# VectorE's turn of an expert loop: weighted rows and the next-but-one tile's first basis placed ahead of the hidden normalisation

## What is computed

```python
logits = x @ gate_W;  rw, sel = top_k(softmax(logits), 2);  rw = rw / rw.sum(-1)
# experts 0 to 3, "plain"
mlp_out = gelu(x @ mlp_W1 + b1) @ mlp_W2 + b2
# experts 4 to 7, "KAN"
basis0 = rswaf(layernorm(x), grid)          # 8 grid points: 1 - tanh(..)^2
z      = basis0 @ kan_sl_W0 + b0            # 128*8 -> 256
basis1 = rswaf(layernorm(z), grid)          # 256*8
kan_out = basis1 @ kan_sl_W1 + b1           # -> 128
out = sum over experts of w_full[t, e] * expert_out[e, t]
```

## Time and profile before

| | us |
|---|---|
| median of 3 runs (952.75, 953.87, 958.70) | 953.87 |
| the profiled execution | 949.07 |
| its span, first to last instruction | 947.2 |
| mean granted TensorE clock | 0.954 of full speed |

### The profile page before, as it was taken

How to read it: one execution, slowest core, us unless ns; L and a number is a source line. 1 busy time by engine, 2 the same in 40 slices (tenths; PEclk the granted TensorE clock), 3 DMA queues, 4 the chain that set the end, 5 groups by cost and what they waited for, 6 DMA issues and landing times.

```text
span 947.2 us, 23326 instructions
## 1 busy us (share of the span) xinstructions
PE 814.1 (86%) x7978; PEld 627.7 (66%) x7979; DVE 501.0 (53%) x2069; ACT 548.8 (58%) x731; POOL 505.6 (53%) x649
## 2 busy tenths in 40 slices
PE   3699897998979989789896889999889899899980
PEld 1456675666656766657675668888668698677870
DVE  6734726547356373563744664565635845576240
ACT  6566664666656666566565463764835737556330
POOL 6240624546246361463547377676867767766522
PEclk9799998999999999999999989999999999899985
DMA  3302040130401303103047062552634525424213
GB/s 74 97 32 68 2 132 1 36 98 2 130 3 36 98 2 106 26 22 112 2 127 150 19 158 42 135 139 38 135 92 79 138 33 136 120 51 69 21 18 106
DMA packets 91065, 68.24 MB, mean 72 GB/s; under 512 B 42894, under 2 KB 83276, under 8 KB 89038
## 3 DMA queue, kind: packets, MB, share of 16 engines
q1 hardware_dynamic: 74014, 55.11, 20.7%
q0 software_dynamic: 16912, 11.35, 8.5%
HBM read 46.86 MB, written 21.37 MB: 72 GB/s over the span
## 4 chain that ended last, share of the span: by engine, by line
PE 38%; POOL 25%; issue 14%; DVE 9%; ACT 4%; DMA 4%; another core or an unknown queue 1%; SPq 1%; POOLq 1%; DVEq 1%; ACTq 0%
POOL acc_d L752 8%; PE pv L1636 7%; PE pv L1532 5%; PE ring L1598 4%; PE ring L1602 4%; DVE masked L1185 3%; POOL vaug L742 3%; POOL stack L742 3%; PE ring L1498 3%; DMA acc_d<-stack,srec 2%; PE ring L1557 2%; PE ring L1416 2%; ACT Pb L927 2%; POOL zc L768 2%; POOL c L668 2%
## 5 line engine op out<-in xcount | busy, mean ns | idle before, releaser
L752 POOL DMA_INDIRECT acc_d<-stack,srec x84 | 166.6, 1983 | 82.2 <-DVE stack L1104 55.6
L1185 DVE CUSTOM_DVE_ANT_0 masked<-ring,mask_max 128x192 bf16<-128x192 f32 (+1 forms) x512 | 141.2, 337 | 99.1 <-PE ring L1557 87.0
L933 ACT ACTIVATE Pb<-ring 128x768 f32<-128x768 f32 x128 | 101.2, 812 | 78.4 <-PE ring L1586 67.6
L780 POOL TENSOR_SCALAR_AFFINE_SELECT Pb<-Pb 128x1024 f32<-128x1024 f32 x64 | 69.0, 1096 | 125.0 <-ACT Pb L927 124.8
L1116 DVE SCALAR_TENSOR_TENSOR stack<-stack 128x512 f32<-128x512 f32 x160 | 102.1, 688 | 58.3 <-ACT stack L906 55.6
L1498 PE MATMUL ring<-stack 128*128 128x256 f32 x560 | 124.1, 381 | 0.0
L1636 PE MATMUL pv<-Pb,vaug 128*32 128x128 f32 (+3 forms) x2816 | 119.2, 318 | 0.0
L809 POOL DMA_INDIRECT slot_d<-rec,pos x64 | 62.4, 976 | 105.1 <-DVE pos L1287 87.7
L1498 PEld LDWEIGHTS ring<-stack 128*128 128x128 f32 x560 | 105.4, 190 | 19.0 <-issue 5.2
L906 ACT ACTIVATE stack<-ring,kprm 128x512 f32<-128x512 f32 x160 | 108.2, 813 | 0.1
L943 ACT ACTIVATE Pb<-ring 128x768 f32<-128x768 f32 (+1 forms) x128 | 89.0, 758 | 27.7 <-PE ring L1602 26.2
(11 more groups left out here) (243 smaller groups left out, 1374.1 us busy)
## 6 DMA issues: line engine op xcount, KB each, us to landing
stack<-L_ffn_kan_sl_W SPq DMA_DIRECT2D x20, 1024.0 KB, 5.7
stack<-hl_d SPq DMA_DIRECT2D x24, 256.0 KB
stack<-hl_d SPq DMA_DIRECT2D x24, 128.0 KB
stack<-L_ffn_mlp_W SPq DMA_DIRECT2D x12, 256.0 KB
hl_d<-hi SPq DMA_DIRECT2D x7, 384.0 KB, 2.6
hl_d<-lo SPq DMA_DIRECT2D x7, 384.0 KB, 3.5
Pb<-L_ffn_mlp_W SPq DMA_DIRECT2D x10, 256.0 KB
xb<-L_attn_x SPq DMA_DIRECT2D x9, 256.0 KB, 4.7
```

The costliest lines, as they stand in the source:

```text
L752: pool.indirect_dma_start(acc_d, bass.IndirectOffsetOnAxis(ap=srec[:, kind, u % RECS, q, 0:1], axis=0), src[:, u % 2, q, :], None, compute ...
L933: act.activation(Pb[:, n % 2, 2048 + 768 * hd:2048 + 768 * (hd + 1)].rearrange("p (k q) -> p k q", k=2), slot(job)[:, :, 0:384], ACT.Squar ...
L1185: red = dve.tensor_tensor_reduce(masked[:, (NT * n + c) % SLOTS, hh, k0:WQ], slot(job)[:, hh // 2, WQ * (hh % 2) + k0:WQ * (hh % 2 + 1)], ...
```

## The change

VectorE's list of a turn is put in another order, and nothing else: `hidden_norm` of KAN tile u+1 moves behind `weighted(0, ...)` of u+1 and `basis_functions(0, ...)` of u+2, under a condition of its own, so each turn has one condition more on VectorE.

```diff
                         with dve.If(k + 1 < n_kind[1]):
                             hidden_stats(i, u + 1)
-                            hidden_norm(i, u + 1)
                         with dve.If(k + 1 < n_kind[0]):
                             weighted(0, i, u + 1)
                         with dve.If(k + 2 < n_kind[1]):
                             basis_functions(0, i, u + 2)
+                        with dve.If(k + 1 < n_kind[1]):
+                            hidden_norm(i, u + 1)
                         with dve.If(k < n_kind[1]):
                             weighted(1, i, u)
```

## The result

The changed kernel takes 923.42 us (median of 4 runs, 920.82 to 925.51), the kernel before 956.24 with one more run counted, 4 in all (952.75 to 958.70): a ratio of 0.9649, 95% interval 0.9614 to 0.9683, or 33 us less. The profiled execution went from 949.07 to 920.82, 28.2 less, and its span from 947.2 to 919.0. The forecast was 926 us for the median and 919 for the span.

The account below looks back on a forecast made before the run. GpSimd's list was taken to pace turns 3 to 8. A loss of 31.4 us, less 1.8 for short turns and 1.6 for transfers and holds, gave 28 us: profiled 949.07 becomes 921, median 926, range 918 to 940 for eight in ten.

Parts of the forecast that it names:

- The bound before: GpSimd's instruction list, a round of 38.3 us gather to gather, paces turns 3 to 8, which total 230.7 us.
- The sum of 31.4: Turns 1 to 8 took 299.3 us against TensorE's need of 267.9; the 31.4 us loss lies nearly all in turns 3, 4, 5, 7, 8.
- The wait, 3.6 a round: GpSimd's 3.89 us wait for the weighted plain rows shrinks to the usual 0.30 gap, 3.6 us less per round.
- the hold, 3.9 a round: GpSimd's first scatter, held by VectorE's gapless first basis, falls from 5.50 to some 1.6 us, 3.9 less per round.
- The gapless basis in turns 3 and 6: There the first basis stays gapless and holds GpSimd's coefficients or gather, up to 4.4 us, once each.
- Rival A: The hold only moves to a gather or the coefficients; only the wait goes, 21.6 us less, 932 us; chance 0.17.
- TensorE becomes the bound: GpSimd's new round of 30.8 us falls below TensorE's need of 33.3 a turn in turns 3 to 8; clock 1.00.
- need of 267.9: TensorE's own work in turns 1 to 8, summed from fixed matmuls and KAN and plain blocks, 267.9 us.
- short turns, landings and holds: Deductions from the gain: 1.8 us in the two short turns, some 1.6 for transfers and holds longer than 0.1.
- The heads: TensorE's waits at turn heads, 1.91 us for weighted rows and 2.57 for Gelus, both go with the earlier basis.
- The room of the normalisation: Time between the later `hidden_norm` and TensorE's need at the next head; short turns 4 and 7 (-1.2, -0.6) lose 1.8 us.
- rival B: Basis steps each wait for a GpSimd gather or scatter, some 10 us a turn; 975 us, break-even about 7.4; chance 0.06.

Follow-up runs that it names:

- the pair with less matmul: 2 of 16 steps of the second KAN product left out, in the changed order and in the old one: turns 1 to 8 262.8 and 293.6 us.
- gaps_half_weights: Kernel before, with one-element stores between first-basis steps and half of each KAN weight load left out: 278.3 us in turns 1 to 8, ratio 0.9747.
- change_again: The whole change timed again on another chip against the kernel before: 994.16 us against 1021.49, ratio 0.9737, turns 1 to 8 270.1 us.
- The delay experiment: Changed kernel with nine extra VectorE instructions (3.06 us) ahead of each normalisation: 276.8 us in turns 1 to 8, ratio 0.9823 against the kernel before.

## Why the prediction was right

- **The bound before.** GpSimd's round paced turns 3 to 8: right for turns 2 to 7, by the pair with less matmul (0.5 us of 221) and by gaps_half_weights, less so for turn 8.
- **The cuts of the earlier trace rows.** From turn 4 on some cuts lie where TensorE ran out of work and not at the next head: turns 4, 5 and 7 begin at 698.66, 736.91 and 814.57, 2 to 4 us later. Turn 6 was therefore read as fully busy, and it wasn't: 4.23 us of waiting stood at its end. The sum of 31.4 doesn't change by this, only its split over the turns.
- **The wait, 3.6 a round, and the hold, 3.9 a round.** Both went: 0.7 for 3.89, 1.6 to 2.0 for 5.50. The gap left is 0.7 and not 0.3.
- **The gapless basis in turns 3 and 6.** It held one coefficient 4.2 us in turn 6. In turn 3 it held nothing to its end: the coefficients took 0.32 to 0.52 beside it. So my reading of the hold, that it lasts as long as the run is gapless, is right for the scatters and too simple for the coefficients. Rival A's mechanism was there once, without a price, as TensorE had room.
- **TensorE becomes the bound, at full clock.** 268.8 us against a need of 267.9. The 31.4 held both the waits and the slow clock behind them, and both went. The loss left was mis-sized: I had 31.4 - 28 = 3.4 us for short turns, landings and holds, and 0.9 was paid (2.2 in change_again, 1.6 of it at the heads behind the short turns, where I had 1.8). So the loop gained 30.5, and 2 us were lost ahead of turn 1, half of them in turn 0, which I had let keep its time; their cause is open. That the profiled execution came out at 920.82 for a forecast of 921 is luck to that extent: two errors of some 2 us cancel. The median then stood 2.6 above it and not 4.8.
- **The heads.** TensorE's waits for Gelus, 8.6 us in turns 1 to 8 before, are gone, and ScalarE's wait for the basis fell from 64.0 us to 1.4.
- **The room of the normalisation.** Foreseen 6.8, 3.3, 2.9, -1.2, 5, 2.6, -0.6 for turns 1 to 7; the trace after has 6.9, 3.4, 5.3, -0.2, 7.0, 4.4, -0.3. The delay experiment paid exactly where this says. The break-even of rival B was not tried; by the rooms of the prediction it comes to 7.0 us, not 7.4.
- **Rival B fell.** Basis steps of the same kind took 660 to 722 ns, though they now lie beside GpSimd's gathers and scatters; before it was the earlier trace rows. The Trainium skill's rule that the prediction names beside this rival, that the one that issued first keeps the ports, is not borne out for VectorE here: no step waited for a scatter of 1.6 to 2 us.

```profile
L1116 DVE SCALAR_TENSOR_TENSOR stack<-stack x160: 660/692/722, 507.1 to 874.1; 128x512 f32<-128x512 f32 x160
```

- **What I did not see.** The sum treated wait and hold as two terms that add up. They don't: the two halves of the reordering gave 12.4 and 0.5 us alone, together 30.5, and the hold taken away by stores gave 9.1. Two ties were missing. The weighted rows also release TensorE's next head, so the basis early is of no use while they are late. And the plain scatter lands behind the weights, so a shorter round on GpSimd ran into that wait. With the whole change the plain scatters are issued before the weights of their turn, or within 0.3 us of them, in turns 1 to 7 except turn 6 (median 3.4 us from issue to landing, 7.9 at most), and TensorE's own need capped the gain. So the total came out though the terms by themselves were wrong.

## What to carry to other kernels

When an order written by hand is changed, ask of each instruction who waits for it on all engines, and put first what releases another engine's list; what only has room to the next turn's head goes last. A stall of one engine beside a gapless run on another may be dissolved, as here, with a tiny instruction between the steps, but look first at what the stall covers. Count a wait of TensorE with the slow clock behind it: here 19.4 us of waits saved brought 11.1 more. Two halves of a reordering can each be worth little and the whole a lot, so test the whole before dropping a half.

## What the runs showed of the hardware that I had not expected

A one-element store of 0.06 us between VectorE's basis steps lets GpSimd's indirect transfers through (5.50 us becomes 1.89), and the steps still begin every 0.61 us instead of every 0.60. Without it a scatter was held in all 23 gapless runs that met one first, and a coefficient in 2 of 7.

The same kernel before took 950 to 1038 us on the chips used. Turns 1 to 8 are alike on them (270.1 for the change against 268.8), and the part before isn't: turn 1 began at 593.27 on one chip and at 664.2 on another, and turn 0 took 45.3 us on the one and 52.7 on the other. The stretch from 400 to 500 us, after on the first chip, then change_again on the other, the same columns as above:

```profile
400.00:500.00 100.00, 90.98 (x1262) 66.19 (x1259) 56.96 (x341) 63.18 (x87) 48.23 (x74) 1.00 0.23 62
```

```profile
400.00:500.00 100.00, 82.88 (x971) 58.35 (x968) 48.98 (x297) 51.15 (x69) 38.23 (x57) 0.93 0.16 44
```

The second gets through 971 matmuls at a granted clock of 0.93 where the first gets through 1262 at 1.00, though by then the two are no longer at the same place in the program. Why was not tried. The longer total explains only a small part of the step from 3.5% on one chip to 2.6% on the other; the rest is the 33 us against 27.3, which is open.
